# A two-norm block with a feed-forward network on 8 cores: four pairs of the first half's gate and up products as seven block products, the first half's tokens kept in device memory meanwhile

## What is computed

```python
def _layernorm(x, axis=-1, eps=1e-5):
    m = jnp.mean(x, axis=axis, keepdims=True)
    v = jnp.var(x, axis=axis, keepdims=True)
    return (x - m) / jnp.sqrt(v + eps)

def attn(x, bind_key, unbind_key, gate, decay):
    bound = circ_conv(x, bind_key)                       # along the 1024 features
    decay_matrix = where(t >= s, sigmoid(decay) ** (t - s), 0)
    hologram = einsum('ts,bsd->btd', decay_matrix, bound)
    return x + gate * circ_corr(hologram, unbind_key)

def ffn(x, w_gate, w_up, w_down):                        # int32 weights, scale 1/127
    gate = einsum('bsd,hd->bsh', x, wg)                  # h = 3072
    up   = einsum('bsd,hd->bsh', x, wu)
    return einsum('bsh,dh->bsd', silu(gate) * up, wd)

x = x + layernorm(attn(layernorm(x), ...))
x = x + layernorm(ffn(layernorm(x), ...))
```

## Time and profile before

| | before |
|---|---|
| median of 3 runs | 578.94 us (578.37 to 579.88) |
| the profiled execution | 579.18 us; span of its slowest core 576.8 us |
| spans of the eight cores | 575.2 to 576.8 us |
| PE busy | 558.6 us, 97% of the span, 2708 matmuls |
| DVE, POOL, ACT busy | 322.0, 262.9, 181.4 us |
| share of the chain that ended last | PE 88%, DVE 4%, issue 3%, DMA 2%, POOL 2%, ACT 1% |

### The profile page before, as it was taken

How to read it: one execution, slowest core, us unless ns; L and a number is a source line. 1 busy time by engine, 2 the same in 40 slices (tenths; PEclk the granted TensorE clock), 3 DMA queues, 4 the chain that set the end, 5 groups by cost and what they waited for, 6 DMA issues and landing times.

```text
span 576.8 us, 8369 instructions; the slowest of 8 cores (575.2 to 576.8 us)
## 1 busy us (share of the span) xinstructions
PE 558.6 (97%) x2708; PEld 255.7 (44%) x2708; DVE 322.0 (56%) x507; ACT 181.4 (31%) x251; POOL 262.9 (46%) x432
## 2 busy tenths in 40 slices
PE   8789999999999999999999999999999999999994
PEld 3444444444444444444444444444444444444442
DVE  3887747676546511113243268898998987223222
ACT  3566751144223521122332323233333232001011
POOL 2677773356314511000111679989999970001010
PEclk9999999999999999999999999999999999999998
DMA  7972119666728398400026914444655400000101
GB/s 209 339 158 49 28 28 145 102 98 105 104 44 129 64 157 124 76 0 37 36 59 129 179 74 68 79 73 74 100 92 98 76 1 2 36 37 36 74 37 73
DMA packets 14203, 49.51 MB, mean 86 GB/s; under 512 B 1744, under 2 KB 3152, under 8 KB 13392
## 3 DMA queue, kind: packets, MB, share of 16 engines
q0 software_dynamic: 8544, 31.46, 34.5%
q1 hardware_dynamic: 5328, 17.45, 8.6%
q10 hardware_dynamic: 288, 0.07, 0.1%
HBM read 72.04 MB, written 8.39 MB: 139 GB/s over the span
## 4 chain that ended last, share of the span: by engine, by line
PE 88%; DVE 4%; issue 3%; DMA 2%; POOL 2%; ACT 1%; DVEq 0%; POOLq 0%; ACTq 0%; SPq 0%
PE pb L524 14%; PE pa L524 13%; PE pc L711 11%; PE pa L711 11%; PE pa L804 7%; PE pb L711 7%; PE pc L804 7%; PE pb L804 7%; PE psc L804 4%; PE pc L382 2%; DMA x<-xin 2%; PE pc L308 1%; PE pt L474 1%; DVE sta L248 1%; PE pc L372 1%
## 5 line engine op out<-in xcount | busy, mean ns | idle before, releaser
L253 POOL TENSOR_SCALAR r<-mv 128x1 f32<-128x1 f32 x32 | 6.7, 209 | 185.5 <-DVE mv L724 167.9
L524 PE MATMUL pa<-x2t,wgu 128*128 128x512 f16 x384 | 87.6, 379 | 0.9 <-ACT sil L532 0.8
L524 PE MATMUL pb<-x2t,wgu 128*128 128x512 f16 x384 | 87.8, 379 | 0.0
L711 PE MATMUL pa<-wd,h 128*128 128x512 f16 x276 | 61.5, 379 | 0.0
L711 PE MATMUL pc<-wd,h 128*128 128x512 f16 x276 | 61.5, 379 | 0.0
L524 PEld LDWEIGHTS pa<-x2t,wgu 128*128 128x128 f16 x384 | 37.0, 98 | 44.7 <-issue 1.8
L524 PEld LDWEIGHTS pb<-x2t,wgu 128*128 128x128 f16 x384 | 37.1, 98 | 42.8
L732 DVE SCALAR_TENSOR_TENSOR x<-v,gf,x 128x1024 f32<-128x1024 f32 (+1 forms) x17 | 21.6, 1278 | 39.7 <-ACT v L730 39.7
L258 POOL TENSOR_TENSOR r<-r,nhf 128x1 f32<-128x1 f32 x64 | 36.9, 576 | 9.5
L711 PE MATMUL pb<-wd,h 128*128 128x512 f16 x184 | 41.0, 379 | 0.0
L711 PEld LDWEIGHTS pa<-wd,h 128*128 128x128 f16 x276 | 26.9, 98 | 31.9
(11 more groups left out here) (187 smaller groups left out, 907.8 us busy)
## 6 DMA issues: line engine op xcount, KB each, us to landing
wgu<-wgu POOLq DMA_DIRECT2D x24, 512.0 KB, 7.2
wp<-wgu POOLq DMA_DIRECT2D x22, 512.0 KB, 8.9
x<-xin SPq DMA_DIRECT2D x16, 512.0 KB, 8.0
out<-x SPq DMA_DIRECT2D x15, 512.0 KB, 2.6
wd<-wdt POOLq DMA_DIRECT2D x6, 1024.0 KB, 14.2
wph<-wgu POOLq DMA_DIRECT2D x2, 512.0 KB, 10.3
out<-x SPq DMA_DIRECT2D x2, 256.0 KB, 2.1
hkf<-hki SPq DMA_DIRECT2D x1, 394.5 KB, 7.6
```

Of the source, the lines that this page charges most:

```text
L524: tok = P.put("tensor", lambda e_, d=d: e_.matmul(ten[:, 512 * half:512 * half + 512], WGU[s][:, 1024 * half + 128 * d:1024 * half + 128 * ...
L711: tok = P.put("tensor", lambda e_, fc=fc, e=e: e_.matmul(pair[:, 512 * fc:512 * fc + 512], (H, HB)[hf][e][:, 128 * tl:128 * tl + 128], WD[ ...
```

## The change

Hidden tiles 0 to 15 of the first half stay as slots (8 to 31 in the loop). Tiles 16 to 23 become four pairs, k = 8 to 11, by the same `pair` as in the second half, now with the half as its first argument. To make room, each token tile `X[0]` to `X[7]` is copied to device memory (`xsp`) after its `x1_op`, by a DMA on SP's queue, and copied back after pair 11. The token differences of the first half (`TA_`) lie in `X[0]` to `X[3]`, the weight sums in `X[4]` to `X[6]`; four new pairs of weight buffers (`WA`) lie in free places, one of them in the fifth part of `WD`. So the loads of the last two parts of `WD` are put behind pair 8, and the other four are spread over slots 11 to 23.

The helper functions move up in the file and take the half `hf`; their arithmetic is as it was. The core of the diff:

```diff
+    xsp = nc.dram_tensor("xsp", [8, 128, 1024], F32)
...
-        for e in range(NSLOT, NH):
+        for e in range(NSLOT, 16):
             for c in range(2):
                 yield e, c
...
+    spill = [P.dma("sync", xsp[t, :, :], X[t][:], f"sp{t}", x1[t]) for t in range(8)]
+    gone = lambda t: [spill[t], x2[t], sqx[t]]
...
-            if e in (3, 6, 9, 12, 15, 18):
+            if e in (5, 7, 9, 11):
                 load_wd(len(wd_tok))
+
+    put_at(20, 1, lambda: load_pair(0, 8, tk["gp"]))
+    put_at(24, 1, lambda: load_pair(0, 10, scan[3], gone(7)))
+    put_at(25, 1, lambda: load_one(0, 9, 0, scan[3]))
+    put_at(27, 1, lambda: load_one(0, 9, 1, upend[13]))
+    put_at(29, 1, lambda: load_one(0, 11, 0, upend[14]))
+    put_at(31, 1, lambda: load_one(0, 11, 1, upend[15]))
+    for i in range(4):
+        put_at(19 + 2 * i, 1, lambda i=i: token_sums(0, i, [gone(j) for j in range(4)]))
+    put_at(27, 0, lambda: weight_sums(0, 8, gone(4), gone(5), ms=(0,)))
+    put_at(29, 0, lambda: weight_sums(0, 8, gone(4), gone(5), ms=(1,)))
+    put_at(31, 0, lambda: weight_sums(0, 9, gone(5), gone(6), ms=(0,)))
+    put_at(32, 0, lambda: weight_sums(0, 9, gone(5), gone(6), ms=(1,)))
...
+    def rest8():
+
+        for key in sorted(work):
+            for fn in work[key]:
+                fn()
+        use[("u3", 0)] = sqx[15]
+
+    late.append(rest8)
...
+    for k in range(8, 12):
+        pair(0, k)
+        if k == 8:
+            load_wd(5)
+            weight_sums(0, 10)
+            load_wd(4, pend[(0, 8)])
+        if k == 9:
+            weight_sums(0, 11)
+    late.pop(0)()
+    back = [P.dma("sync", X[t][:], xsp[t, :, :], f"rl{t}", spill[t], pend[(0, 11)]) for t in range(8)]
...
             fin[t] = P.put("vector", lambda e, lo=lo, hi=hi: e.scalar_tensor_tensor(
-                X[t][:, lo:hi], o[:, lo:hi], GF[:, s], X[t][:, lo:hi], ALU.subtract, ALU.add), y, g)
+                X[t][:, lo:hi], o[:, lo:hi], GF[:, s], X[t][:, lo:hi], ALU.subtract, ALU.add), y, g, back[t] if t < 8 else None)
```

More of the change, by code:

```diff
@@ L467, in x2_op @@
             i = ORD2.index(t)
-            old = x2t[ORD2[i - 1]] if i else sqx[15]
+            old = x2t[ORD2[i - 1]] if i else [sqx[15], use[("u3", 0)]]
         x2[t] = P.put("scalar", lambda e: e.activation(
@@ new lines, in build_nc, with block @@
+    BK = {"pa0": PA[:, 0:512], "pa1": PA[:, 512:1024], "pb0": PB[:, 0:512], "pb1": PB[:, 512:1024],
+          "pc": PC[:, 0:512], "pc1": PC[:, 512:1024], "ps": PS[:]}
+    ring = ["pc", "pc1", "ps", "pa0", "pa1", "pb0", "pb1"]
+    silp = [None] * 4
+    use = {}
+    UPS = INV127 * INV127
+    def block(hf, k, m, p, key, first, fin_):
+        S = WS[k % 2][m]
+        raw = {1: (0, 0), 2: (0, 512), 4: (1, 512), 7: (1, 0)}.get(p)
+        col = {5: 0, 6: 512, 3: 1024}.get(p)
+        mv = {1: (X2T, 1024, 0), 2: (X2T, 1024, 4096), 3: (X2T, 1024, 4608)}.get(p) or TS[hf][p]
+        need = [wpair[(hf, k, 0)], wpair[(hf, k, 1)],
+                evt[8 * hf:8 * hf + 4] if p in (1, 2) else (evt[8 * hf + 4:8 * hf + 8] if p == 3 else tsum[hf]),
+                ssum[(hf, k, m)] if p in (3, 5, 6, 7) else None]
+        for d in range(4):
+            w = S[:, col + 128 * d:col + 128 * d + 128] if raw is None else wcol(hf, k, raw[0], 1024 * m + raw[1] + 128 * d, 128)
+            tok = P.put("tensor", lambda e, d=d, w=w: e.matmul(
+                BK[key], w, mv[0][:, mv[1] * d + mv[2]:mv[1] * d + mv[2] + 512], start=(first and d == 0),
+                stop=(fin_ and d == 3), skip_group_check=True), need, free[key], sig=(d == 3))
+        return tok
@@ L754, in build_nc @@
[L754 to L799, removed]
-        need = [wpair[(k, 0)], wpair[(k, 1)], evt[8:12] if p in (1, 2) else (evt[12:16] if p == 3 else tsum),
-                ssum[(k, m)] if p in (3, 5, 6, 7) else None]
-        for d in range(4):
-            w = S[:, col + 128 * d:col + 128 * d + 128] if raw is None else wcol(k, raw[0], 1024 * m + raw[1] + 128 * d, 128)
-            tok = P.put("tensor", lambda e, d=d, w=w: e.matmul(
-                BK[key], w, mv[0][:, mv[1] * d + mv[2]:mv[1] * d + mv[2] + 512], start=(first and d == 0),
-                stop=(fin_ and d == 3), skip_group_check=True), need, free[key], sig=(d == 3))
-        return tok
```

235 lines of the change are left out of this document (138 added, 97 removed).

## The result

The changed kernel takes **580.75 us** (median of 20 runs, 578.96 us the lowest), the kernel before 579.17 us in the runs beside it (also 20). The ratio is 1.002, with a 95% interval of 1.0011 to 1.0028: slower by 1.6 us, less than the 0.3% that the prediction set as its bound for no change. The forecast was 579.1 us. So 32 matmuls were taken away and nothing was gained. In absolute time the median lies 0.05 us above 580.7 us, the upper end of what the prediction called its own forecast. The profiled execution has spans of 575.4 to 578.7 us, before 575.2 to 576.8.

What follows compares the result with a forecast made beforehand. PE bounds the kernel: matmul count times their distance, plus PE's waits. Terms -6.1 + 4.6 + 1.7 = +0.2 us took the profiled 579.18 to 579.4, 579.1 us as a median; 8-in-10 range 575.3 to 581.8.

Steps and rivals of the forecast that it cites:

- its own forecast: The main case, gain and waits about equal: 577.2 to 580.7 us, likeliest 579.1, chance 0.48.
- four pairs at 12.28 us instead of 16 slots: First half before the downs: four pairs take 49.13 us where 16 slots took 55.26, saving 6.1 us.
- PE waits around pair 8: PE waits 4.6 us before pair 8's seventh block, partly perhaps at its start, for DVE's late `part`; ends 2.4 and 6.3.
- pair 9's fifth block waits for sums: PE waits 1.7 us there for POOL's sums, ready at 218.4 us but due at 216.8; ends 0 and 2.
- copies, late down weights: Token-tile copies out and back and the down weights' fifth part cost 0; holding up the downs had chance 0.02.
- the clock in the wait: Rival: clock halves during PE's pair 8 waits, slowing blocks; 581 to 582.5 us, chance 0.25 with the waits' upper ends.
- POOL's walk: POOL's queue, slots 27 to 31: rounds of 11.15 us against PE's 8.63, so tile 15's power ends at 204.15 us.
- S: POOL's price for half a pair's weight sums, four additions: taken as 5.45 us, ends 4.68 and 5.83.
- (3): Sign: PE idle before pair 8's seventh block, released by DVE's `part`, 3 to 5 us together with the pair's start.
- (4): Sign: PE idle before pair 9's fifth block, released by POOL's sums, 1 to 2 us.
- (5): Sign: whether the granted clock stays at 1.00 from 196 to 215 us, left open.
- (6): Sign: the downs do not wait for `x` or `wd`.

Runs made afterwards that it cites:

- e10: Changed kernel with pair 8's weight sums in slot 22, its load at slot 17, and first-half token differences two slots earlier: 573.39 us, kernel before 578.92.
- e3: Kernel before with only the eight copies to device memory and back added, no first-half pairs: 586.09 us, kernel before 585.92 on the same chip.
- e6: The changed kernel run again, unaltered, on another chip: 586.95 us, kernel before 586.29 on that chip.
- e9: Changed kernel with only the four groups of first-half token differences two slots earlier: 580.08 us in one run, kernel before 578.92.
- e4: Changed kernel with the first addition in each half of pair 8's sums made three times on POOL: 594.06 us, kernel before 585.92.

## Why the prediction was right, point by point

| step | predicted | measured |
|---|---|---|
| four pairs at 12.28 us instead of 16 slots | -6.1 | pairs 10 and 11: 12.33 and 12.26; e10: -5.8 with a wait of 0.37 |
| tile 15's power on POOL | 204.15 us | 204.23 us on core 0 (203.66 + 0.57), 203.8 on the mean |
| first `part` of pair 8 done | 206.4 us | 207.0 us |
| PE waits around pair 8 | +4.6 | 5.1 (idle by the profile 1.62 + 3.18, means of eight cores) |
| pair 9's fifth block waits for sums | +1.7 | 0.17 where the clock held, none where it fell |
| a `part` late inside pair 9 | not named | +0.37 |
| copies, late down weights | 0 | copies 0.6 by e3's steady cores; no wait of the downs |
| the clock in the wait | a rival, +2 | +1.6 on 3 of 8 cores in the profile |

**The gain** was right in kind and size: without the waits a stretch of four pairs takes 49.45 us (e10, 0.37 of idle in it), and 49.13 was said.

**POOL's walk** was right in its rounds to a tenth of a microsecond. S was 5.4 us where 5.45 was taken, and the round 11.1 where 11.15 was. The start of the walk was 0.2 us off: the token differences moved tile 13's power by 0.4 us against the slots, and 0.6 was said. Its rows came from the second half's sums beside DVE, and the same pattern stands here (1.95 us for the second addition).

**The wait of pair 8** lies where the prediction put it: partly at the pair's start, mostly before the seventh block. Its size takes a word on reading. The profile counts idle time from the end of the last matmul, which is modelled, and here that end stands 0.16 us behind the moment at which the next matmul would start. On core 4, 16 matmuls from 192.78 us on, 0.216 us apart, make pair 8 due at 196.24 us; it starts at 198.04, and the seventh block starts 3.35 us after it is due. PE loses 5.15 us there, and 5.1 on the mean of the cores, where the idle times add up to 4.8. The term of 4.6 was 0.5 us too small. The first `part` was done 0.6 us late because `x1_op` took 2.08 us. The prediction had both its prices and took the short one, though POOL's next sums start 0.15 us before it. It also took 5.32 us for six blocks, which take 5.18. The 0.3 us by which POOL was ahead of the walk took some of this back.

**The start of pair 8** was due 0.7 us later than before on the mean of the eight cores, 196.4 us against 195.7. The forecast has no term for that, and most of it is scatter. On the mean 0.6 us of it are there at 29 us, with -0.4 to +2.0 on single cores, and the first copy is issued only at 31 to 33 us. In e6, the same kernel on another chip, pair 8 was due 1 us earlier on the mean of the steady cores. The remaining 0.1 us are small gaps in slots 27 to 30 that the prediction gave as free. On core 0 two parts of slots stand 3.74 us apart, where 3.45 are needed:

```profile
184.67 3.62 PE L530 MATMUL pb<-x2t,wgu 128*128 128x512 f16 x16
188.41 3.61 PE L530 MATMUL pa<-x2t,wgu 128*128 128x512 f16 x16
```

**The wait of pair 9 was wrong**, and it is the step that failed. It was to be 1.7 us and is 0.17. Two parts of it: the second half's sums took 4.6 us, not 5.45, since by then no `x1_op` ran beside them (1.15, 1.16, 1.16 and 1.16 us each on core 0), and POOL began them at 212.32 us on core 4, where the walk gives 204.15 + 5.45 + 0.64 + 2.66 = 212.9. They were done at 216.94 there, not at 218.4, and the block was due at 217.1. The prediction's own numbers, 218.35 less 216.78, give 1.6 and not 1.7. The price S held for a half that starts together with an `x1_op`, and the prediction used it for one that doesn't. With the 0.37 us of a `part` in pair 9 the term is 0.5 instead of 1.7.

**The clock.** A core that holds its clock should spend 49.45 + 1.80 + 3.35 + 0.17 = 54.8 us from the due start of pair 8 to the downs, and core 4 does (196.24 to 251.00), against 55.26 before. That is 0.5 us less. With the later start and the 0.3 us more behind the first down it comes out level: the five cores that held have spans of 576.3 us on the mean, the kernel before 576.0. A core whose clock falls has 1.6 us more, and in the profiled execution one such core is the slowest. The rival was right in its mechanism and its place. It priced the fall at four blocks and 3.5 us, 2 us after what pair 9's wait takes in; it was two blocks and 1.6 us in this execution, with next to nothing to take in. Its point of decision, about 2 us of standstill, was not tested: the waits at the pair's start were shorter (1.4 to 1.7 us, no fall), and even 3.2 us left the clock up on five cores.

**Why the number was near.** In part by luck. The waits were 0.7 us lower than forecast in sum (5.1 + 0.5 against 4.6 + 1.7), the start was 0.7 us later, the stretch behind the first down 0.3 us longer, and the clock, which the forecast left to a rival, added 1.6. The sum of +0.2 becomes +2.1 for a core that falls, against the mean core of before. The three that fell have 578.4 us on the mean, 2.4 over 576.0; from slowest core to slowest core it is 1.9 us (578.7 against 576.8), and between the medians 1.6.

**The signs that were listed.** (1) 2676 matmuls, as said. (2) tile 15's power at 204.2 us, DVE idle 2.80 and 2.97 us before the last two `x1_op`, as said. (3) as said. (4) 0 to 0.17 us, not 1 to 2. (5) the clock is not at 1.00 on three cores. (6) no wait of the downs; the last part of the down weights was issued at 228.7 us where 230 was said. The first down starts between 250.06 and 253.26 us, inside 249 to 254.

## What to carry to other kernels

Work that nobody urgently waits for should not be put into an in-order queue ahead of small operations on which a chain of another engine hangs; here 11 us of additions cost 5 us of PE, and the same additions five slots earlier, in the queue's idle stretch, cost nothing. Before moving work to an engine, walk its queue once around with durations from rows that have the same neighbours, and compare the round with the bounding engine's: 11.1 against 8.6 us told nearly all. And where a wait of about 3 us on TensorE can't be removed, what the clock does after it is part of its price, on the slowest of all cores.

## What the runs showed of the hardware that was not expected

The same wait on the same program did not always bring the clock down. After waits of 3.17 to 3.21 us it fell on 3 of 8 cores in the changed kernel, on 3 of the 4 steady cores in e6 and on 5 of 8 in e9; after waits of 3.5 to 4.3 us on all four steady cores of e4, both times; after waits of up to 1.7 us never. The length of the wait does not tell the cores that fell from the others, and they were others in each run: 0, 6 and 7, then 4, 5 and 6, then 0 to 3 and 5. Nor does the fall have to come while PE stands still. On core 7 of the changed kernel the seventh block still runs at the full level, and the clock comes down behind it:

```profile
206.97 1.02 PE L637 MATMUL pc<-ta,wa 128*128 128x512 f16 x4 [3.17 <-DVE u L644]
207.83 1.57 PE L637 MATMUL pb<-ta,ws 128*128 128x512 f16 x4
```

What decides it stays open. A fall cost 1.6 us in most cases and 2.8 us in two, on core 3 of e9 and core 1 of e4. The dearer kind seems not to be rare: core 3 of e9 has a mean clock of 0.990, and in 9 of the changed kernel's 20 executions the slowest core has 0.989 or 0.990 and a span of 579.2 to 579.9 us, where in the profiled one it has 0.994 and 578.7. So the traces read here show a milder execution than the median. Since the slowest of eight cores counts and each of these three runs had several that fell, a wait of 3.2 us costs this kernel about 4.8 us, its length and 1.6, and more where a core falls for longer.
